# Linear attention reordered in three engines, and constants built later: a fused decoder layer in float32

## What is computed

```
h = ln1(x);  q, k, v = h@wq, h@wk, h@wv                 # linear attention
phi(a) = elu(a) + 1 = max(a + 1, min(exp(a), 1))
x1 = x + (phi(q) @ (phi(k)^T v)) / (phi(q) . sum phi(k) + 1e-6) @ wo    # per sequence and head
x  = ln(x + x1 + lookup_gelu(ln2(x1) @ w1) @ w2)        # feed-forward, inner width 512
x  = ln(x + softmax(mask(x@WQ, ctx@WK)) (ctx@WV) @ WO)  # causal cross attention
x  = ln(x + x@W_shared^T + (top-2 weights) * x@W_expert^T + bias)
```

## Time and profile before

| what | value |
|---|---|
| median of 3 runs | 599.19 us (598.56 to 599.45) |
| the profiled execution | 602.87 us, its span 601.2 us |
| busy: PE, DVE, ACT, POOL | 527.9, 416.3, 369.0, 330.8 us |
| linear attention, one steady step | 6.87 us, PE busy in 6.26 of them |
| feed-forward, one steady step | 7.45 us, PE busy throughout |
| first work on PE (turned rows of group 0) | 9.70 us after the span's start |
| last `kv_products` of linear attention | 125.78 us |

### The profile page before, as it was taken

The page is one execution under the profiler, slowest core; times in us unless marked ns, Lnnn a source line. Parts: engine busy times, 40 slices in busy tenths (PEclk is TensorE's granted clock), DMA queues, the critical chain, the costliest instruction groups (busy, mean ns, idle before and its releaser), DMA issues.

```text
span 601.2 us, 22996 instructions
## 1 busy us (share of the span) xinstructions
PE 527.9 (88%) x9312; PEld 370.4 (62%) x9312; DVE 416.3 (69%) x1453; ACT 369.0 (61%) x643; POOL 330.8 (55%) x603
## 2 busy tenths in 40 slices
PE   2699998989999999988999999998989989999741
PEld 1467776656677767755666666666646656666530
DVE  2567777766767765375587778777867787779743
ACT  2356566557777777766766666666656666666520
POOL 6766667745755556341337554655465447554563
PEclk9899999999999999999999999999999999999876
DMA  5610000000000001001112111111111011111001
GB/s 160 188 38 3 3 1 2 3 3 1 1 2 1 2 5 26 1 11 28 27 32 49 29 40 33 49 30 43 29 48 28 27 48 50 28 34 22 20 19 35
DMA packets 24986, 17.97 MB, mean 30 GB/s; under 512 B 3120, under 2 KB 21424, under 8 KB 24880
## 3 DMA queue, kind: packets, MB, share of 16 engines
q1 hardware_dynamic: 24448, 16.43, 10.4%
q10 hardware_dynamic: 432, 0.07, 0.1%
HBM read 9.67 MB, written 4.19 MB: 23 GB/s over the span
## 4 chain that ended last, share of the span: by engine, by line
PE 58%; SPq 9%; ACT 8%; DVE 7%; issue 7%; POOL 6%; DMA 4%; POOLq 0%; DVEq 0%; ACTq 0%
SPq L394 8%; PE pair L1145 7%; PE pair L1179 7%; PE pair L1194 6%; PE pair L1213 6%; PE pair L1258 5%; PE pair L1114 5%; PE pair L1223 4%; PE pair L1036 4%; DMA k_exp<-k_sb 3%; ACT gel L718 3%; PE pair L1107 3%; PE pair L1232 2%; PE pair L1201 2%; PE pair L1049 2%
## 5 line engine op out<-in xcount | busy, mean ns | idle before, releaser
L718 ACT ACTIVATE gel<-pair 128x1024 f32<-128x1024 f32 x64 | 65.5, 1024 | 75.4 <-PE pair L1213 75.4
L926 DVE TENSOR_REDUCE neg_max<-pair 128x16 f32<-128x1024 f32 x64 | 60.9, 951 | 20.3 <-PE pair L1201 20.2
L1194 PE MATMUL pair<-k_exp,qT 64*32 64x256 f32 (+1 forms) x1024 | 57.5, 501 | 8.5 <-DMA k_exp<-k_sb 7.7
L1179 PEld LDWEIGHTS pair<-w,gel 128*128 128x128 f32 x512 | 60.3, 192 | 7.4 <-issue 5.5
L1223 PEld LDWEIGHTS pair<-v,gel 128*32 128x32 f32 x4096 | 41.7, 110 | 37.1 <-ACT gel L718 31.2
L1179 PE MATMUL pair<-w,gel 128*128 128x128 f32 x512 | 62.2, 276 | 1.0 <-ACT gel L643 1.0
L1223 PE MATMUL pair<-v,gel 128*32 128x18 f32 x4096 | 48.2, 187 | 15.5 <-ACT gel L718 12.8
L1145 PE MATMUL pair<-hT,w 128*128 128x512 f32 x128 | 58.5, 597 | 1.9 <-ACT lev L638 1.3
L712 ACT ACTIVATE gel<-gel,row_scale 128x512 f32<-128x512 f32 x80 | 54.4, 719 | 4.8 <-DVE gel L939 4.8
L303 POOL TENSOR_SCALAR veps_c<-mv_c 128x4 f32<-128x4 f32 x16 | 3.7, 229 | 96.0 <-issue 89.8
L303 POOL TENSOR_SCALAR veps_b<-mv_b 128x4 f32<-128x4 f32 x32 | 7.8, 245 | 81.6 <-DVE mv_b L295 45.8
(11 more groups left out here) (127 smaller groups left out, 1228.5 us busy)
## 6 DMA issues: line engine op xcount, KB each, us to landing
X<-in_x SPq DMA_DIRECT2D x16, 256.0 KB, 3.0
cT<-in_ctx SPq DMA_DIRECT2D x16, 256.0 KB, 2.9
out_rows<-X SPq DMA_DIRECT2D x16, 256.0 KB, 2.5
k_exp<-k_sb SPq DMA_DIRECT2D x160, 16.0 KB
w<-in_L_attn_w SPq DMA_DIRECT2D x2, 256.0 KB, 3.3
w_kv<-in_L_attn_wk SPq DMA_DIRECT2D x1, 64.0 KB, 3.2
w_q<-in_L_attn_wq ACTq DMA_DIRECT2D x1, 64.0 KB, 3.0
w_kv<-in_L_attn_wv SPq DMA_DIRECT2D x1, 64.0 KB, 3.1
```

The costliest lines, as they stand in the source:

```text
L718: nc.scalar.activation(pT[par], pair[par][:, :, :].rearrange("p a c -> p (a c)"), ACT.Copy).then_inc(pT_ready, 1)
L926: nc.vector.tensor_reduce(neg_max[par][:, :].rearrange("p (a h) -> p a h", a=2), scores, AX.X, ALU.max, negate=True).then_inc(max_ready, 1)
L1179: last = nc.tensor.matmul(bank(6 + q)[:, P * t:P * (t + 1)], gel[:, q, f, P * t:P * (t + 1)], w_2[:, f, :], start=(f == 0), stop=(f == NF ...
L1194: nc.tensor.matmul(pair[t % 2][b * QW:(b + 1) * QW, half, 0:HH * width], qT[p][rows, batch + first:batch + first + QW], keys, start=True, ...
```

## The change

Four edits.

- PE, phase 1: the rows of group s + 2 are turned ahead of the products of k and v, no longer behind them.
- ACT, phase 1: h of group s + 2 (`rows_h`, `rows_h2`) is made ahead of k's exponential and v's copy, no longer behind them.
- DVE, phase 1: the order is `kv_sum(s)`, `attend(s)`, phi_q(g), minimum and phi_k(g), and the statistics come last and one group further on (s + 4 instead of s + 3; the statistics of group 2 stay in the first step).
- The constants that POOL built between groups 1 and 2 are cut into five parts (`late_constants`), one behind each of the steps 3 to 7 of the feed-forward, and DVE's `constants()` moves from behind step 7 to behind step 11. At the start of the cross attention ACT runs `probabilities(0)` ahead of `rows_a` of group 13, and `rows_a` of groups 14 and 15 after the slots 1 and 2 instead of before the slots 0 and 1.

```diff
--- before.py
+++ after.py
@@ -433,6 +433,31 @@
                 ln_rows_pool(pool, ln2, g, lambda t: X1[:, g * TG + t, :],
                              lambda t: xn[p][:, t, :], mv[p], negm, rstd[p])
 
+            def late_constants(part):
+                if part == 0:
+                    const(nc.gpsimd.memset(half_mask[:, :], 1.0))
+                    for b in range(2):
+                        m = half_mask[b * S:(b + 1) * S, :]
+                        const(select(out=m, in_=m, compare_op=ALU.is_ge, fill=0.0, base=0,
+                                     pattern=[[-DH, HH]], channel_multiplier=1))
+                        const(select(out=m, in_=m, compare_op=ALU.is_ge, fill=0.0, base=DH - 1,
+                                     pattern=[[DH, HH]], channel_multiplier=-1))
+                if part == 1:
+                    const(nc.gpsimd.memset(causal[:, :, :], 0.0))
+                if part in (1, 2):
+                    b = part - 1
+                    c = causal[b * S:(b + 1) * S, :, :]
+                    const(select(out=c, in_=c, compare_op=ALU.is_ge, fill=NEG, base=S - QW,
+                                 pattern=[[0, HH], [-1, S]], channel_multiplier=1))
+                if part in (3, 4):
+                    i = part - 3
+                    const(nc.gpsimd.memset(v2[i][:, :, :, :, :], 0.0))
+                    for h in range(2):
+                        const(nc.gpsimd.memset(v2[i][h * S:(h + 1) * S, :, :, h, DH:HV], 1.0))
+                    const(nc.gpsimd.memset(moe_out[i][:, :, 2 * D + NE:], LOWEST))
+                if part == 4:
+                    pool.sem_inc(const_ready)
+
             select = nc.gpsimd.affine_select
             nc.gpsimd.memset(minus_half[:, :], -0.5)
             nc.gpsimd.memset(minus_one[:, :], -1.0)
@@ -452,26 +477,6 @@
                 const(nc.gpsimd.memset(heads[:, :, :, DH:HV], 1.0))
                 pool.sem_inc(const_ready)
                 rows1(i, i)
-            const(nc.gpsimd.memset(causal[:, :, :], 0.0))
-            const(nc.gpsimd.memset(half_mask[:, :], 1.0))
-            for b in range(2):
-
-                m = half_mask[b * S:(b + 1) * S, :]
-                const(select(out=m, in_=m, compare_op=ALU.is_ge, fill=0.0, base=0,
-                             pattern=[[-DH, HH]], channel_multiplier=1))
-                const(select(out=m, in_=m, compare_op=ALU.is_ge, fill=0.0, base=DH - 1,
-                             pattern=[[DH, HH]], channel_multiplier=-1))
-
-                c = causal[b * S:(b + 1) * S, :, :]
-                const(select(out=c, in_=c, compare_op=ALU.is_ge, fill=NEG, base=S - QW,
-                             pattern=[[0, HH], [-1, S]], channel_multiplier=1))
-            for i in range(2):
-                const(nc.gpsimd.memset(v2[i][:, :, :, :, :], 0.0))
-                for h in range(2):
-                    const(nc.gpsimd.memset(v2[i][h * S:(h + 1) * S, :, :, h, DH:HV], 1.0))
-                const(nc.gpsimd.memset(moe_out[i][:, :, 2 * D + NE:], LOWEST))
-            pool.sem_inc(const_ready)
-
             def phase1(s, p):
                 if exists(s - 2):
 
@@ -553,7 +558,11 @@
             for s in range(2):
                 zero(k_exp[s])
 
-            pipeline(pool, phase2, first=2, last=NG - 4)
+            for s in range(2, NG - 3):
+                phase2(s, s % 2)
+                if 3 <= s <= 7:
+                    pool.wait_ge(ln_a.offs, 2 * s)
+                    late_constants(s - 3)
             pool.wait_ge(w_loaded, ALL_WEIGHTS)
             spread_k(0, 0)
             phase2(NG - 3, 1)
@@ -613,23 +622,24 @@
                     act.wait_ge(negq_ready, g + 1)
                     nc.scalar.activation(expqk[q][:, 0, :], expqk[q][:, 0, :], ACT.Exp,
                                          scale=-1.0).then_inc(expq_ready, 1)
-                    act.wait_ge(kv_done, g + 1)
-                    after(act, phik_ready, g - 1)
-                    kv = pair[3][:, :, :].rearrange("p a (t c) -> p (a t) c", c=2 * D)
-                    nc.scalar.activation(expqk[q][:, 1, :].rearrange("p (t d) -> p t d", d=D),
-                                         kv[:, :, 0:D], ACT.Exp).then_inc(expk_ready, 1)
-
-                    after(act, kvsum_done, g - 1)
-                    nc.scalar.activation(
-                        v_ext[q].rearrange("p t (h e) -> p t h e", e=HV)[:, :, :, 0:DH],
-                        kv[:, :, D:2 * D].rearrange("p t (h e) -> p t h e", e=DH), ACT.Copy)\
-                        .then_inc(v_ready, 1)
                 if exists(s + 2):
                     rows_h(s + 2, p)
                 if second_norm(s + 2):
                     if s + 2 == NG:
                         act.wait_ge(w_loaded, ALL_WEIGHTS)
                     rows_h2(s + 2 - NG, p)
+                if exists(g):
+                    act.wait_ge(kv_done, g + 1)
+                    after(act, phik_ready, g - 1)
+                    kv = pair[3][:, :, :].rearrange("p a (t c) -> p (a t) c", c=2 * D)
+                    nc.scalar.activation(expqk[q][:, 1, :].rearrange("p (t d) -> p t d", d=D),
+                                         kv[:, :, 0:D], ACT.Exp).then_inc(expk_ready, 1)
+
+                    after(act, kvsum_done, g - 1)
+                    nc.scalar.activation(
+                        v_ext[q].rearrange("p t (h e) -> p t h e", e=HV)[:, :, :, 0:DH],
+                        kv[:, :, D:2 * D].rearrange("p t (h e) -> p t h e", e=DH), ACT.Copy)\
+                        .then_inc(v_ready, 1)
 
             def quantise_even(s, f):
 
@@ -772,13 +782,14 @@
             nc.scalar.preload_act_table(ACT.Exp)
             act.wait_ge(const_dve, 5)
             act.wait_ge(const_ready, 3)
+            probabilities(0)
             rows_a(NG - 3, 1)
-            probabilities(0)
+            act.wait_ge(down_done, NG)
+            phase3(0, 0, slots=(0, 1))
             rows_a(NG - 2, 0)
-            act.wait_ge(down_done, NG)
-            phase3(0, 0, slots=(0,))
+            phase3(0, 0, slots=(2,))
             rows_a(NG - 1, 1)
-            phase3(0, 0, slots=range(1, TG))
+            phase3(0, 0, slots=(3,))
             pipeline(act, phase3, first=1, last=NG + 1)
 
 
@@ -858,10 +869,10 @@
                 g, q, r = s + 1, 1 - p, s - 2
                 if exists(s):
                     kv_sum(s, p)
-                if exists(s + 3):
-                    statistics1(s + 3, 1 - p)
-                if second_norm(s + 3):
-                    statistics2(s + 3 - NG, 1 - p)
+                if s < 0:
+                    statistics1(2, 0)
+                if exists(s):
+                    attend(s, p)
                 if s == NG - 1:
                     quantise_odd(0, 1)
                 if exists(g):
@@ -869,9 +880,6 @@
                     after(dve, num_done, g - 1)
                     nc.vector.scalar_tensor_tensor(phi_q[q][:, :], bank(1), 1.0, expqk[q][:, 0, :],
                                                    ALU.add, ALU.max).then_inc(phiq_ready, 1)
-                if exists(s):
-                    attend(s, p)
-                if exists(g):
 
                     dve.wait_ge(expk_ready, g + 1)
                     nc.vector.tensor_scalar(expqk[q][:, 1, :], expqk[q][:, 1, :], 1.0, None, ALU.min)\
@@ -884,6 +892,10 @@
                         phi_k[q][:, :, :], kv[:, :, 0:D], 1.0,
                         expqk[q][:, 1, :].rearrange("p (t d) -> p t d", d=D), ALU.add, ALU.max)\
                         .then_inc(phik_ready, 1)
+                if exists(s + 4):
+                    statistics1(s + 4, p)
+                if second_norm(s + 4):
+                    statistics2(s + 4 - NG, p)
 
             def phase2(s, p):
                 g, q, r = s + 1, 1 - p, s - 1
@@ -1016,9 +1028,9 @@
 
 
             pipeline(dve, phase1, last=NG - 1)
-            pipeline(dve, phase2, first=0, last=NG // 2 - 1)
+            pipeline(dve, phase2, first=0, last=NG - 5)
             constants()
-            pipeline(dve, phase2, first=NG // 2, last=NG - 1)
+            pipeline(dve, phase2, first=NG - 4, last=NG - 1)
             phase3(-1, 1, slots=(2, 3))
             phase2(NG, 0)
             phase3(0, 0)
@@ -1108,6 +1120,10 @@
                         .then_inc(q_done, 1)
                 if exists(s):
                     numerators(s, p)
+                if exists(s + 2):
+                    xpose_rows(s + 2, p)
+                if s + 2 == NG:
+                    xpose_rows2(0, p)
                 if exists(g):
                     after(pe, phik_ready, g)
                     for t in range(TG):
@@ -1115,10 +1131,6 @@
                             pair[3][:, t // 2, 2 * D * (t % 2):2 * D * (t % 2 + 1)],
                             hT[q][:, P * t:P * (t + 1)], w_kv[:, :], start=True, stop=True)
                     last.then_inc(kv_done, 1)
-                if exists(s + 2):
-                    xpose_rows(s + 2, p)
-                if s + 2 == NG:
-                    xpose_rows2(0, p)
```

(7 more changed lines are left out.)

4 lines of the change are left out of this document (removed).

## The result

| | kernel before | changed kernel |
|---|---|---|
| median of 20 executions each | 597.49 us (595.40 to 599.46) | 600.93 us; of the 18 undisturbed 600.70 (597.31 to 604.94) |
| ratio, with its 95% interval | | 1.0051 [1.0035, 1.0068] |
| the profiled execution, its span | 602.87, 601.2 us | 604.94, 603.2 us |
| repeated beside the later experiments | 601.41 us | 603.13 us, ratio 1.0019 [0.9997, 1.0041] |

Two executions of the changed kernel, of 1269.7 and 756.81 us, were disturbed and are left out of the ratio. The change makes the kernel slower: by 3.0 us in the first comparison (0.51% of 597.5; 2.1 to 4.1), by 1.1 us in the second (-0.2 to 2.5). The profiled executions differ by 2.1 us. The forecast was +0.9 us. The likeliest class in it was "same" (within 0.2%), with 0.41, and "slower" had 0.33; the first comparison says slower, the second can't tell.

What follows compares the result with a forecast made beforehand. Linear attention was taken as bound by a loop of waits through PE and ACT's h. Terms +0.42 - 2.84 - 1.30 + 4.62 gave +0.9, elsewhere nothing: 603.8 us profiled, 600.1 median, range 595.0 to 602.9.

Steps and rivals of the forecast that it cites:

- h leaves the loop: Linear attention, PE and ACT: the 0.60 wait goes, but phi_k's loop of 6.80 us leaves a gain of 0.06 a step.
- The statistics enter the loop: Linear attention, DVE: statistics between phi_k and `kv_sum`, formerly free, now delay `kv_sum` and make the step 7.22 us.
- The rival in which the statistics don't delay `kv_sum`: Linear attention: statistics slip into `kv_sum`'s wait; step 6.80, 5.4 us less, 593.8 us; chance 0.12.
- statistics beyond it: DVE, linear attention: of 1.50 us of statistics, 1.33 remain between phi_k's end and `kv_sum`'s start.
- `numerators` to the exponential: PE, linear attention: 2.71 from the start of `numerators` to k's exponential plus 0.44 for turned rows, 3.15 us.
- 7.22, between them: Linear attention step, taken between 7.18 and 7.28, for a hand-over to PE of 0.05 or 0.15.
- the rival of the shorter loop: Linear attention: loop shorter than its rows add up to, some 7.0; -2.4, 596.8 us; chance 0.16.
- The start: First linear attention steps: rows no longer late behind the constants, first `kv_products` 0.42 later, next intervals gain 2.84 and 1.30.
- with no clock drop: Start of linear attention: intervals after the first `kv_products` are 7.22 each, without the earlier low clock.
- the rival of the clock: Start of linear attention: granted clock falls once more, costing 1.7 to 3.4, taken 2.6; 602.7 us; chance 0.10.
- The feed-forward: POOL's constants fit into 2.58 us of waiting per step, largest part 2.0, and `constants()` costs nothing; price 0, at most 1.6.
- The cross attention: Its start, ACT: `rows_a` of group 14 makes a copy 0.76 late, swallowed by PE's next wait; price 0, at most 0.8.

Runs made afterwards that it cites:

- e3: Kernel before with only PE's and ACT's parts of the change in linear attention; ratio to before 1.0010 [0.9984, 1.0036].
- e1: Changed kernel with DVE's old order within a step (statistics right behind `kv_sum`, `attend` behind phi_q); ratio to before 0.9959 [0.9931, 0.9988].
- e7: Changed kernel with statistics of group s + 4 right behind `kv_sum`, `attend` behind phi_q, group 3 added in the first step; ratio to before 0.9960.
- e4: Kernel before with only the constants moved (POOL's five parts, DVE's `constants()` four steps later); ratio to before 0.9942, repeated 0.9944.
- e6: Changed kernel with ACT's old order at the start of the cross attention (`rows_a` put back); ratio to before 1.0028 [0.9997, 1.0059].
- e2: Kernel before with only DVE's part (statistics last and for s + 4, `attend` ahead of phi_q); ratio to before 0.9981 [0.9955, 1.0008].
- e9: Changed kernel with the constants and ACT's start of the cross attention put back as before; ratio to before 1.0068 [1.0040, 1.0095].
- e8: e7 with the first step in the old order (turned rows of group 1 and h behind k and v); ratio to before 0.9926, repeated 0.9944.

## Why the prediction came out as it did

**h leaves the loop, and gains almost nothing: right.** Forecast for PE's and ACT's part without the statistics 6.80, a gain of 0.06; e3 has 6.79, e1 6.80. With POOL's rows out of the way it is 6.73 (e7).

**The statistics enter the loop: right, and the step was over-sized.** DVE took its instructions in program order, as the prediction argued from its rows. The Trainium skill ("TensorE: Matmul & The Clock Gate", section "Architectural detail") calls DVE's queue strict first-in first-out; the trace agrees. The rival in which the statistics don't delay `kv_sum` (6.80) is refuted by the rows at 78.18 and 78.48, and e1 shows that they are the cause. The terms, forecast and measured from the rows of the steady step:

| term | forecast | measured |
|---|---|---|
| exponential's start to phi_k's end | 1.89 | 1.86 (75.28 to 76.45 + 0.69) |
| statistics beyond it | 1.33 | 1.34 (77.14 to 78.48) |
| `kv_sum` | 0.76 | 0.73 |
| hand-over from DVE to PE | 0.09 | 0.05 (79.21 to 79.26) |
| `numerators` to the exponential | 3.15 | 3.08 (79.26 to 82.34) |
| step | 7.22 | 7.06 |

The step at fault is the one that took "7.22, between them" and summed rows to 3.15: four terms each 0.03 to 0.07 too long are 0.16 a step and 2.2 us in 14 of them. Part of it is that k and v take 1.89 behind the turned rows, where they took 1.99 behind `numerators`. It is nearly the rival of the shorter loop ("some 7.0").

**The start: the gain was right in kind, and its length was the second mis-sized term.** The constants no longer hold PE (the rows at 23.26 wait for nothing), and e4 shows that this is where the gain lies. But "with no clock drop" failed in this profile and in that of the repeated kernel: the rival of the clock, with a chance of 0.10, happened there, and by e6 its low stretch costs 1.2 us. The argument against it was that the wait before 24.94 was longer. But a wait of 1.98 us ahead of 19.43 was enough, and by itself the length doesn't decide: in e6 PE waited 2.02 us ahead of 18.52 and the clock did not fall. The Trainium skill ("TensorE: Matmul & The Clock Gate", section "The HAM clock gate") has the clock withdrawn in idleness. That the fall followed a wait agrees with it, but which wait brings one, the rows don't show.

The first `kv_products` came 1.04 after the forecast (19.43 against 18.39), and this lies ahead of the fall. "Turning the rows of group 1 ahead of k and v makes the first `kv_products` 0.42 later" took the full rate, but at 13.56 the products still ran at half of it, with the granted clock at 1.00: the rows took 0.86 (13.56 to 14.42), 0.44 more. And k and v of group 0 took 3.03 us, where they had taken 2.39 (at 13.61); that is 0.64 more, and in e6 they took 2.03. The rest is 0.05 of an earlier start. The next interval was 8.30 for 7.22.

**Errors that cancelled.** Against the forecast of 126.69 for the last `kv_products`: +1.04 at the first one, +1.08 in the next interval, -2.15 for 14 steps of 7.067, +0.33 for one step of 7.40. That is +0.3, and it was 127.00. That the sum came out so close is luck: each of the first three is larger than the forecast effect of 0.9.

**The step of 7.40.** PE waits 0.61 instead of 0.27 for `kv_sum` at 107.86, since DVE paused between two bn_aggr. The timeline of DVE:

```profile
106.45 0.18 DVE L295 BATCH_NORM_AGGREGATE mv<-stats 128x2 f32<-128x6 f32 x1 [0.26 <-DVE stats L288]
106.86 0.31 DVE L295 BATCH_NORM_AGGREGATE mv<-stats 128x2 f32<-128x6 f32 x3 [0.23 <-issue]
```

It is the same step in the five profiles with this order (changed, repeated, e2, e6, e9), at five different times, so it belongs to the place in DVE's program. In e2, where the statistics are not on the loop, it costs 0.13 (6.99 against 6.86). The kernel before has a pause at its own place too, 0.63 instead of 0.26 ahead of the bn_aggr at 108.15, and its step stays at 6.86. What DVE does there no row tells.

**The feed-forward: nothing was forecast, -0.3 was measured.** POOL's largest part, 1.8 us long (188.12 to 189.89), lies inside the idle time, and 1.0 remains before POOL needs DVE again. POOL's timeline answers to the earlier trace rows:

```profile
188.12 1.06 POOL L454 MEMSET v<- 128x1152 f32 x1
189.24 0.48 POOL L456 MEMSET v<- 64x64 f32 x2
...
193.55 0.23 POOL L303 TENSOR_SCALAR veps_b<-mv_b 128x4 f32<-128x4 f32 x1 [1.00 <-DVE mv_b L295]
```

The small gain lies where DVE's `constants()` was. Around it PE's steps took 7.60 and 7.54 us (182.03, 189.63, 197.17) and take 7.44 now. "At either place lies under PE's full work" was thus not quite so, but only the second of the two steps holds `constants()` (191.96 to 192.90); in the first a weight load waited 0.18 for h at 189.62, and why h was late there I did not find. From the last `kv_products` to the first `pT` copy it is 136.13 to 136.14 in before, e2, e3 and e9, and 135.80 to 135.90 in the changed kernel, e1, e4, e6, e7 and e8: without and with the move.

**The cross attention: `rows_a` right, +1.0 not foreseen, and not part of the change.** The third copy is 0.55 late and the fourth 0.13 (1.51 and 1.09 after those of before, less the 0.96 of the first). ACT's timeline answers to the earlier trace rows:

```profile
271.43 1.00 ACT L728 ACTIVATE gel<-pair 128x1024 f32<-128x1024 f32 x1
...
276.19 1.02 ACT L728 ACTIVATE gel<-pair 128x1024 f32<-128x1024 f32 x1 [0.30 <-PE pair L1225]
```

What grew from the one profile to the other is the wait of PE for the transfers of `k_exp`. The view of costly groups, whole kernel (busy, mean ns, idle before):

```profile
L1206 PE MATMUL pair<-k_exp,qT 64*32 64x256 f32 (+1 forms) x1024 | 57.6, 501 | 9.4 <-DMA k_exp<-k_sb 9.4
```

It was 7.7 us before. It is 9.4 in e6 too, with ACT's old order, 8.0 in the repeated changed kernel with the new one, and 6.9 to 9.1 in the nine others: it scatters by more than the 1.0 us in question, whatever ACT's order.

The low clock scatters here too. The windows of 2 us of the changed kernel in the tenth step of the cross attention:

```profile
448.00:450.00 2.00, 0.00 (x0) 0.00 (x0) 1.73 (x10) 1.87 (x3) 1.19 (x3) 1.00 0.48 131
450.00:452.00 2.00, 1.76 (x16) 0.26 (x16) 0.02 (x1) 0.00 (x0) 0.00 (x0) 0.55 0.01 2
452.00:454.00 2.00, 2.00 (x24) 1.44 (x17) 1.18 (x1) 0.00 (x0) 0.00 (x0) 0.60 0.00 0
```

PE had waited 2.38 us for `k_exp` until 450.24. Six of the 13 profiles have this fall (before, changed, repeated, e6 and both of e8) and a tenth step of 22.8 to 24.0 us; e7 has one two steps earlier. The six others have none, and a tenth step of 21.2 to 21.7, in e2 19.8, though five of them waited 1.97 to 2.59 us at that place. It costs 1 to 2.7 us, and both kernels of the first pair have it. From the first `pT` copy to the end of the span the 13 profiles take 335.8 to 341.2 us. The changed kernel takes 340.3 in both of its profiles and the one before 339.3, but e1, with the same code there, takes 337.3. So +1.0 is well inside the scatter, and no run shows that the change adds anything here.

**What stays open.** The linear attention accounts for +1.2 us less 0.3 in the profiles; the first comparison measured +3.0 (2.1 to 4.1), the second +1.1 (-0.2 to 2.5). I can name three things that scatter by 1 to 3 us from one execution to the next, the slow products at the start, the waits for `k_exp` and the low clock in the cross attention, but not which value they have in the executions without a profile. The slowdown was measured at 0.5, 0.2 and, with e6's same linear attention, 0.3%. Its parts are +4.2 for the statistics in the loop (e1's profile), -3.4 for the constants (e4's ratio, -2.0 to -4.9), about -1 for h out of the loop (0.07 to 0.08 in 13 steps, e3's profile), and 0 to +2 for the slow products at the start. Added up these are -0.2 to +1.8, which meets the second comparison and not all of the first; e4's interval alone is wide enough for the rest. By the other way, e1's ratio (-2.5 us, -0.7 to -4.1) and the 4.2 on top, it is +1.7, 0.1 to 3.5.

## What to carry to other kernels

- Before taking a wait out of a loop, add up the second longest loop from the same rows. Here it was 0.06 us shorter than the first, so a wait of 0.60 was worth 0.07 (e3); what had been hidden beside that wait, 1.3 us of statistics, then came out 0.2 to 0.3 a step dear.
- An instruction that is free in one place is free because of a certain wait (e2). When that wait is what the change removes, cost the instruction again, and put it where the next wait of its engine is: behind `kv_sum`, one group ahead (e7).
- When parts of a change act on different places, run each alone. One of the parts held the gain (e4), and the others hid it.

## What the hardware showed that I had not expected

- The 1.2 GHz stretch at the start moves and vanishes without a change in the code: 24.9 to 31.7 us before, 20 to 23 in the changed kernel (0.53 and 0.62), none in e6 with the same instructions up to there. With and without it the same code is 1.2 us apart, and 2.1 us with what lies ahead of it. Products can run at half rate while the granted clock still reads 1.00: in all 13 profiles q of group 0 takes 2.07 to 2.08 us between 11.3 and 13.9, against 1.12 later. How long this lasts differs from one execution to the next; k and v at 14.42 took 3.03 us, in e6 2.03 at 14.46.
- The same short low stretch, 3 to 7 us, comes in the middle of the cross attention in seven of 13 profiles, behind a wait of PE of 1.8 to 2.6 us for a transfer, and waits of the same length in other profiles bring none.
- k's minimum on DVE takes 0.43 us alone and 0.59 beside POOL's rows, and the rows 1.74 alone and 1.89 beside it (e7, e1). With the minimum 0.4 us behind the rows' start it is 0.42 and 1.96 (before, e4).
- A pause of DVE of 0.23 us between two bn_aggr comes at one place of its program in every profile of that order.
